# One core, a graph network of two layers: TensorE adds all sixteen terms of four tiles of seven, and two steps of the group behind come later on VectorE

## What is computed

```python
h = 2.0 ** 0.5 * relu(emb @ W1 / 10.0 ** 0.5)                 # 16 numbers for each edge
w = (h @ W2 / 16.0 ** 0.5).reshape(E, 7, 16, 8)                # weights made for each edge
s_out = PW_S * (einsum(xs, wa_s) + einsum(xv, y1, wb_s)); g_out = the same with wa_g, wb_g
v_out = PW_V * (einsum(xs, y1, wc) + einsum(xv, wd) + einsum(xv, y2, W3J121, we))
edge_ftr = concat([tanh(s_out), tanh(g_out)[:, :, None] * v_out]) * norm[:, None]
x = x + segment_sum(edge_ftr, edge_dst)                        # first layer
x = x + attention over the same edges, of layer-normed x       # second layer
```

## Time and profile before

| | us |
|---|---|
| median of 3 runs | 1258.34 (1252.8 to 1259.0) |
| the profiled execution | 1253.9 |
| its span | 1252.1 |
| busy: DVE, POOL, PE, ACT, PEld | 963.5, 839.2, 686.6, 645.6, 543.7 |

### The profile page before, as it was taken

How to read it: one execution, slowest core, us unless ns; L and a number is a source line. 1 busy time by engine, 2 the same in 40 slices (tenths; PEclk the granted TensorE clock), 3 DMA queues, 4 the chain that set the end, 5 groups by cost and what they waited for, 6 DMA issues and landing times.

```text
span 1252.1 us, 14590 instructions
## 1 busy us (share of the span) xinstructions
PE 686.6 (55%) x4324; PEld 543.7 (43%) x4324; DVE 963.5 (77%) x1714; ACT 645.6 (52%) x1657; POOL 839.2 (67%) x796
## 2 busy tenths in 40 slices
PE   1357665857666766566663464555440899940000
PEld 0245553746555555455552232333220898940000
DVE  6489999999998999999955888787888899950000
ACT  1367877777777778687753566665511222200000
POOL 6777777767767677764007877777770477777775
PEclk9877787677877687868675567666765555555555
DMA  3312112123121122221134232232110000000000
GB/s 73 80 27 56 43 42 52 31 52 85 32 58 44 34 51 68 45 56 23 50 102 170 70 96 87 64 97 72 39 30 10 5 12 11 11 10 10 10 10 8
DMA packets 40657, 60.31 MB, mean 48 GB/s; under 512 B 17489, under 2 KB 31077, under 8 KB 40324
## 3 DMA queue, kind: packets, MB, share of 16 engines
q1 hardware_dynamic: 12216, 46.86, 11.6%
q0 software_dynamic: 25184, 12.32, 6.2%
q10 hardware_dynamic: 3180, 0.21, 0.2%
HBM read 40.33 MB, written 19.37 MB: 48 GB/s over the span
## 4 chain that ended last, share of the span: by engine, by line
DVE 40%; POOL 18%; DVEq 13%; issue 10%; PE 9%; ACT 6%; DMA 2%; POOLq 0%; SPq 0%; ACTq 0%
POOL out_dram L666 12%; DVE h1d_or_products L1364 6%; POOL x_rows L631 4%; ACT below L859 3%; DVE h1d_or_products L1350 3%; PE sums L1032 3%; DVE halves_or_steps L1357 2%; POOL agg_or_stacks L657 2%; DVEq L1354 2%; DVE xin L1394 2%; DVE dcen L1389 2%; DVEq L1348 2%; DVEq L1323 1%; DVE h1d_or_products L1451 1%; DVE agg_or_stacks L1341 1%
## 5 line engine op out<-in xcount | busy, mean ns | idle before, releaser
L666 POOL DMA_INDIRECT out_dram<-agg_or_stacks,scatter_index x196 | 195.8, 999 | 110.0 <-issue 61.5
L631 POOL DMA_INDIRECT x_rows<-in_x,src_index x196 | 204.5, 1043 | 96.4 <-issue 49.1
L631 POOL DMA_INDIRECT x_rows<-in_x,dst_index x196 | 218.2, 1113 | 59.8 <-issue 58.2
L657 POOL DMA_INDIRECT agg_or_stacks<-run_sums,sum_row_index x196 | 216.6, 1105 | 60.8 <-issue 56.4
L1364 DVE TENSOR_TENSOR h1d_or_products<-tens,hid 128x768 f32<-128x768 f32 x168 | 155.8, 949 | 11.8 <-PE tens L1026 7.8
L1022 PE MATMUL tens<-w_scalar_stacks,stack_turned 96*128 96x384 bf16 x196 | 65.8, 429 | 100.0 <-DVE h1d_or_products L1364 95.6
L1022 PE MATMUL tens<-w_scalar_stacks,agg_or_stacks 96*128 96x384 bf16 x196 | 66.6, 433 | 95.3 <-DVE h1d_or_products L1364 93.9
L1094 PE MATMUL small<-one_column,halves_or_steps 128*128 128x1 f16 x196 | 37.5, 191 | 104.5 <-ACT below L859 63.9
L769 ACT ACTIVATE h1d_or_products<-tens,hid 128x48 f32<-128x48 f32 x448 | 88.5, 345 | 0.0
L1094 PEld LDWEIGHTS small<-one_column,halves_or_steps 128*128 128x128 f16 x196 | 24.0, 122 | 132.3 <-ACT below L859 80.0
L1032 PE MATMUL sums<-h1d_or_products,ident 128*128 128x192 f32 x448 | 78.9, 330 | 0.0
(11 more groups left out here) (283 smaller groups left out, 2270.9 us busy)
## 6 DMA issues: line engine op xcount, KB each, us to landing
src_everywhere<-src_by_columns SPq DMA_DIRECT2D x14, 896.0 KB, 5.0
xin<-in_x SPq DMA_DIRECT2D x27, 449.5 KB
out_dram<-xin SPq DMA_DIRECT2D x27, 449.5 KB
x_rows<-in_x,src_index POOLq DMA_INDIRECT x196, 3.3
x_rows<-in_x,dst_index POOLq DMA_INDIRECT x196, 3.0
run<-run_sums SPq DMA_DIRECT2D x1, 3136.0 KB, 10.3
agg_or_stacks<-run_sums,sum_row_index POOLq DMA_INDIRECT x196, 2.8
out_dram<-agg_or_stacks,scatter_index POOLq DMA_INDIRECT x196, 2.1
```

The lines of the kernel that those rows point to most:

```text
L631: nc.gpsimd.indirect_dma_start(xs[:, t, side, :], None, x, bass.IndirectOffsetOnAxis(ap=idx[:, t:t + 1], axis=0)).then_inc(s_gath[g % LEAD ...
L657: nc.gpsimd.indirect_dma_start(aggr[:, t, :], None, rs, bass.IndirectOffsetOnAxis(ap=ridx[:, t:t + 1], axis=0)).then_inc(s_rsg[g % LEAD2], 16)
L666: nc.gpsimd.indirect_dma_start(out, bass.IndirectOffsetOnAxis(ap=sidx[:, t:t + 1], axis=0), aggr[:, t, :], None, bounds_check=N - 1, oob_i ...
```

## The change

`halve_rest` and its semaphore are gone. `sum_rest` waits for the multiplies themselves (`s_tfree`, `s_tact`) and adds all sixteen terms of the tiles 3 to 6 on TensorE. `prod` of these tiles is therefore read by TensorE until `sum_rest(g-1)` is done, and VectorE waits for that (`s_sumB`) ahead of `multiply(g, 4)`. `outputs(g-1)` moves from behind `dense_sums` to behind `multiply(g, 2)`, `messages(g-1)` from behind `first_rest` to behind `third_part(g+1)`. `dense_centre` now has a drain ahead of it in every group that has one. On ScalarE, `gates(g-1)` moves behind `second_parts(g+1)` and `stage_emb(g+2)`.

```diff
@@ block.scalar, group
-                if past(g, 0):
-                    gates(g - 1)
-                if next1:
                     second_parts(g + 1)
                 if next2:
                     stage_emb(g + 2)
+                if past(g, 0):
+                    gates(g - 1)
                 multiply(g, b)
@@ block.tensor
-            def sum_tiles(halves, a, b):
-                for j in range(HID // 2):
+            def sum_tiles(terms, n, a, b):
+                for j in range(n):
                     mm = nc.tensor.matmul(sums[:, a * OUTS:b * OUTS].rearrange("p (c o) -> p c o", o=OG), ident[:],
-                                          halves[:, :, j, :], start=(j == 0), stop=(j == HID // 2 - 1))
+                                          terms[:, :, j, :], start=(j == 0), stop=(j == n - 1))
...
-                sum_tiles(first_half, 0, TACT).then_inc(s_sumA, 1)
+                sum_tiles(first_half, HID // 2, 0, TACT).then_inc(s_sumA, 1)
             def sum_rest(g):
-                pe.wait_ge(s_half2, g + 1)
-                sum_tiles(prod[:, 2 * TACT:], TACT, GA).then_inc(s_sumB, 1)
+                pe.wait_ge(s_tfree, (g + 1) * NDV)
+                pe.wait_ge(s_tact, g + 1)
+                sum_tiles(prod[:, 2 * TACT:], HID, TACT, GA).then_inc(s_sumB, 1)
@@ block.vector
-            def halve_rest(g):
-                v.drain()
-                dve.wait_ge(s_tact, g + 1)
-                v.tensor_tensor(prod[:, 2 * TACT:, 0:HID // 2, :], prod[:, 2 * TACT:, 0:HID // 2, :],
-                                prod[:, 2 * TACT:, HID // 2:, :], ALU.add).then_inc(s_half2, 1)
@@ block.vector, group
                 multiply(g, b, 0)
-                if past(g, 0):
-                    halve_rest(g - 1)
                 multiply(g, b, 1)
...
                 if g in SLICE1:
                     dense_sums(SLICE1[g])
+                if next1:
+                    first_rest(g + 1)
+                if g in SLICE1:
+                    v.drain()
+                    dense_centre(SLICE1[g])
+                multiply(g, b, 2)
                 if past(g, 0):
                     outputs(g - 1, 1 - b)
-                if next1:
-                    first_rest(g + 1)
-                if past(g, 0):
-                    messages(g - 1, 1 - b)
-                if g in SLICE1:
-                    if not past(g, 0):
-                        v.drain()
-                    dense_centre(SLICE1[g])
-                multiply(g, b, 2)
                 halve(g)
                 if next1:
                     third_part(g + 1)
+                if past(g, 0):
+                    messages(g - 1, 1 - b)
+                if past(g, 0):
+                    dve.wait_ge(s_sumB, g)
                 multiply(g, b, 4)
...
-            halve_rest(NG - 1)
             outputs(NG - 1, 1)
```

More of the change, by code:

```diff
@@ L385, in build_gnn @@
         s_half = sem("first_tiles_halved")
-        s_half2 = sem("last_tiles_halved")
         s_sumA = sem("first_tiles_summed")
```

## The result

The changed kernel takes 1245.07 us (median of 20 runs, 1242.37 to 1253.14), the kernel before, beside it, 1255.37 (20 runs). The ratio is 0.992 [0.9903, 0.9937]: 0.8% faster. I had forecast 1248. The profiled execution has a span of 1241.6 us against 1252.1.

A forecast was written before the change was run, and what follows sets the result against it. VectorE was taken to set the pace of the loop. Full groups −15.6, group 26 −0.2, g mod 4 = 3 −0.6, g mod 4 = 0 nothing, the end +5.8: −10.5 us, from 1258.3 to 1248; range 1221 to 1281.

The forecast's parts named there:

- The sum: All groups' terms added: −10.5 us on the profiled execution, 1248 us on the median of three; chance 0.42.
- The last group and its end: Group 27 up to the read of the sums: 25.9 us against 20.1 before, +5.8.
- Full groups: 13 groups with g mod 4 1 or 2: head 11.0 plus tail 9.9, 20.9 us for 22.1, −15.6 in all.
- the stall of 0.3 in front of `multiply(g, 1)`: Product 1 must wait for `multiply(g-1, 6)` to leave the buffer: 0.3 us at the lower clock, nothing at full.
- the ring: Tail, from multiply 2: outputs, gates, ScalarE's scalings, then product 5, 5.35 us; through product 0, 4.55 more: 9.9 us.
- No new ring: Rival: VectorE keeps the pace throughout, −50 us, 1208 us; chance 0.08.
- TensorE's head: Multiply 0 to 2, ended last by TensorE in g mod 4 = 0 or 3: 10.3 us, between 9.8 and 12.1.
- Its return early in the head: TensorE's clock, low in the tails, returns to full early in the head, which was given 10.3 us.
- The slower rival: Rival: sums become the path at the lower clock, heads 12.1 us; 20 such heads, +20.5, 1279 us; chance 0.22.
- The first rival: Rival: TensorE stays at full clock, −32 us, 1226 us; chance 0.18.
- sign of being wrong: Wrong if VectorE stays busy 93% of the loop, or clock under 0.77 and VectorE awaits product 2 in full groups.
- Gathers: Rival: GpSimd's gathers become late, taking back 13 us at 0.5 a group: 1261 us, no change; chance 0.10.

The follow-up runs named there:

- e4: Changed kernel with ScalarE's scalings of tile 3 ahead of the gates and an early one-column tanh: 1270.45 us, ratio 1.0139 to the kernel before.
- e2: Changed kernel with `halve_rest` back on VectorE and eight terms on TensorE, in the new order: 1264.95 us, ratio 1.0084 to the kernel before.
- e10: Changed kernel with eight of the sixteen terms of tiles 3 to 6 left out, also of the output: 1243.9 us, ratio 0.9875 to the kernel before.
- e1: Changed kernel with eight idle matmul calls (16 instructions) on TensorE between products 4 and 5: 1228.79 us, ratio 0.9807 to the kernel before.
- e3: Kernel before with `halve_rest` dropped and sixteen terms summed on TensorE, nothing moved: 1247.03 us, ratio 0.9944 to the kernel before.
- e9: Changed kernel with the edits of e4 and e1 together, scalings first and idle matmuls: 1269.83 us, ratio 1.0109 to the kernel before.

## Why the prediction was right, step by step

**The sum.** It forecast −10.5 us for the profiled execution; the span fell by 10.5. That is closer than the terms deserve. Groups 1 to 26: −16.97, forecast −16.4. The last group and its end: 27.3 us for 20.1, +7.2, forecast +5.8: its head began low and took 11.6 where I had 9.85, and from M to the read it was 15.7 for 16. Group 0: D of group 1 is 0.7 earlier, forecast nothing. The errors cancel, and that is luck.

**Full groups** −18.1 over thirteen, forecast −15.6. VectorE's head is 10.72 to 10.77 us in the undisturbed ones, against "10.8 to 11.1": the stall of 0.3 in front of `multiply(g, 1)` did not come, since product 1 ran at full clock there (0.90 us from multiply 0 to 1). It did come, 0.34 us, where the head began low. The tail is 9.70, forecast 9.9, and it is VectorE's own work (forecast 9.6) and not the ring: neither in this tail nor in that with g mod 4 = 0 does VectorE wait for a product. So in the 13 groups that brought most of the gain VectorE still sets the pace from end to end, as the rival *No new ring* has it, and an undisturbed one fell from 22.13 to about 20.5.

**The ring** has the timing that I gave it. From M to product 5 it is 5.22 us (371.69 to 376.91), forecast 5.35; from product 5 to the end of product 0 4.53, forecast 4.54. But it ends the tail only with g mod 4 = 3, by the 0.97 us of VectorE's wait for product 6: there the tail is 9.8, and 8.65 in e4, which takes the ring apart, while the other tails differ by 0.15 or less. That `second_parts` and `stage_emb` find their inputs early held in the changed kernel, where the gate waited for `vmix`, and not in e2 and e10, where they and the table load held it back.

**TensorE's head** was taken at 10.3 in the twelve others. It is 9.94 in all six with g mod 4 = 3 (−3.2 us, forecast −0.6), and 11.6 to 11.7 in five of the six with g mod 4 = 0 (+5.0, forecast nothing). VectorE's waits for product 2 are there, 1.1 to 1.4 us in all twelve. The two bounds, 9.8 and 12.1, were nearly met; the split between them was a guess. That the mean of the twelve, 10.7, came near 10.3 is luck.

**The clock.** "Its return early in the head" is what the windows show for g mod 4 = 0 and, earlier, in the tail of the others. The slower rival needed eight low heads of 26 to eat the gain; six of those 26 began low, five of them with g mod 4 = 0, the kind that I had priced at no change, and each of these had a head 1.7 to 1.8 us longer than at full clock (the sixth, group 9, 1.2). The first rival, full clock throughout, was 1226; brought about in e1 it is 1228.79. Neither sign of being wrong showed: VectorE is busy 86% of the loop, not 93, and the clock is 0.82, above 0.77.

**Gathers** were not late: GpSimd's gather has a mean of 352.53 / 346 = 1.02 us, where it was 1.09, and it waited for products as before. With L1350 went the slow gathers beside it: 38 gathers of the loop took over 1.5 us before, 16 do now. Both traces show where the slow ones lie. Beside `halve_rest` and `halve`, which read SBUF twice, the 57 gathers that had begun first take 0.94 us; the 58 that began within such an instruction take 1.2 to 2.2 and end 0.81 to 0.83 us after it, every one.

**No ring** forecast 50 us and is excluded by the twelve other groups and the end, where VectorE waits for product 2 (34.1 us for all products, 6.7 of them in the last group). The 94.3 us of product 5 do not exclude it, since VectorE hardly waits for them.

**What I did not see**: that the order was worth so little (e3), and that the place of the low stretch, not its length, decides (e4, e9). In both I had argued from group lengths at one clock. Nor did I see how few tails the ring would end: I added it up and did not ask in which kinds of group VectorE would wait for it.

## What to carry to other kernels

Work moved from the pacing engine to one with slack is worth its time only until the receiving engine ends some stage, and that is read per kind of group, not over the loop: here 49 us of VectorE's time bought 10.5. A wait of the receiving engine is no sign of it: TensorE waited 94.3 us for ScalarE, and the pacing engine felt it in six groups only. Where TensorE ends a stage, look at the granted clock of just that stage and at the rests in front of it; here idle matmuls in a rest that it had anyway gained more than the change itself (1.1% for 0.8); in e9, where e4's order opened rests elsewhere, they gained nothing clear. An edit that shortens one rest moves the others, so cut the clock by windows again before you count on it.

## What the runs showed of the hardware that I had not expected

Sixteen idle matmul instructions a group (2.00 us of work in a rest of 3.46) took the granted clock over the loop from 0.83 to 0.98, and all but one of 27 heads then began at full clock. Taking sixteen instructions of the sums away lowered it, 0.83 to 0.76 in e10. Between two kernels the clock over the loop can rise from 0.79 to 0.90 (e4 to e9) with the time the same within 0.3%, while the low stretch still covers the head. A gather of GpSimd that began within a VectorE instruction with two inputs on SBUF ended 0.81 to 0.83 us behind it, 58 times of 58, and the 57 that had begun before it took 0.94 us as elsewhere.
